# Attention scores over 32 rows per pair of heads, two pairs side by side, masks two units in a row, eight score buffers

## The reference

```
x = x + Wproj . softmax(mask(q k / 4)) v + bproj      q from layernorm(x), k and v from ctx, 16 heads of 16
x = x + out_proj(ssm(silu(conv(in_proj(layernorm(x))))) * silu(z))     a selective scan, state 16, 512 channels
x = x + down(quant(silu(gate) * up))                   gate, up, down with ternary weights, inputs rounded to 127 steps
```

## Time and profile before

| | us |
|---|---|
| median of 3 runs (lowest, highest) | 548.01 (546.25, 551.74) |
| the profiled execution's own time | 548.35 |
| its span | 546.3 |
| PE busy, share | 454.2, 83% |
| DVE busy, share | 404.0, 74% |
| POOL busy, share | 301.4, 55% |
| ACT busy, share | 246.4, 45% |

### The profile page before, as it was taken

How to read it: one execution, slowest core, us unless ns; L and a number is a source line. 1 busy time by engine, 2 the same in 40 slices (tenths; PEclk the granted TensorE clock), 3 DMA queues, 4 the chain that set the end, 5 groups by cost and what they waited for, 6 DMA issues and landing times.

```text
span 546.3 us, 9183 instructions
## 1 busy us (share of the span) xinstructions
PE 454.2 (83%) x3133; PEld 322.9 (59%) x3138; DVE 404.0 (74%) x779; ACT 246.4 (45%) x539; POOL 301.4 (55%) x310
## 2 busy tenths in 40 slices
PE   4999999999999797656696879998699989575563
PEld 1677777877767563345463647666578766453332
DVE  1376666767669898236979887798887799958994
ACT  1256546465764434582332446738243451223331
POOL 0564866747565625209763557799776689401100
PEclk9999999999999798977788899999799999998877
DMA  8910101101000000082000000173000000000000
GB/s 298 397 41 2 40 1 41 38 2 40 2 1 0 2 1 2 14 246 71 0 1 0 1 0 24 38 175 99 0 2 1 1 0 1 2 1 19 20 20 19
DMA packets 22769, 22.72 MB, mean 42 GB/s; under 512 B 1058, under 2 KB 20258, under 8 KB 22212
## 3 DMA queue, kind: packets, MB, share of 16 engines
q1 hardware_dynamic: 22164, 21.65, 12.5%
q10 hardware_dynamic: 560, 0.50, 0.3%
HBM read 21.03 MB, written 1.12 MB: 41 GB/s over the span
## 4 chain that ended last, share of the span: by engine, by line
PE 36%; POOL 19%; DVE 19%; issue 17%; ACT 3%; DMA 2%; DVEq 0%; POOLq 0%; SPq 0%; ACTq 0%
POOL both L1556 14%; PE ps L474 8%; DVE both L1281 5%; PE ps L483 4%; PE ps L538 3%; PE ps L511 3%; PE ps L714 3%; PE ps L704 3%; PE ps L499 3%; POOL both L1544 2%; PE ps L732 2%; DVE f_s L1381 2%; PE ps L378 1%; PE ps L570 1%; DVE both L1115 1%
## 5 line engine op out<-in xcount | busy, mean ns | idle before, releaser
L1556 POOL TENSOR_TENSOR both<-both 128x1024 f32<-128x1024 f32 x64 | 152.0, 2390 | 69.6 <-DVE both L1281 69.5
L1281 DVE TENSOR_TENSOR_SCAN both<-both,ps 128x1024 f32<-128x1024 f32 x64 | 145.1, 2280 | 33.0 <-PE ps L714 25.1
L945 ACT ACTIVATE both<-delta,a_neg 128x504 f32<-128x504 f32 x128 | 79.4, 706 | 52.1 <-DVE both L1281 52.0
L704 PE MATMUL ps<-both 64*128 64x256 f32 x512 | 77.6, 425 | 29.9 <-DVE both L1281 17.2
L844 ACT ACTIVATE both<-both,negmax 128x256 f32<-128x256 f32 x128 | 63.8, 502 | 65.3 <-DVE negmax L1115 65.2
L1505 POOL TENSOR_SCALAR both<-both,rden 128x256 f32<-128x256 f32 x128 | 63.7, 512 | 48.3 <-DVE rden L1122 48.0
L714 PE MATMUL ps<-con,both 128*128 128x128 f32 x512 | 74.2, 291 | 6.5 <-POOL both L1556 6.5
L704 PEld LDWEIGHTS ps<-both 64*128 64x128 f32 x512 | 47.5, 198 | 51.6 <-DVE both L1281 27.7
L714 PEld LDWEIGHTS ps<-con,both 128*128 128x128 f32 x512 | 58.3, 147 | 29.1 <-issue 15.8
L474 PE MATMUL ps<-both 128*128 128x256 f32 x256 | 70.4, 399 | 3.8 <-POOL both L1494 3.5
L1115 DVE CUSTOM_DVE_ANT_0 both<-ps,both 128x256 f32<-128x256 f32 x128 | 49.0, 420 | 16.7 <-PE ps L474 15.5
(11 more groups left out here) (130 smaller groups left out, 653.4 us busy)
## 6 DMA issues: line engine op xcount, KB each, us to landing
both<-bounce SPq DMA_DIRECT2D x16, 512.0 KB, 5.5
both<-in_ctx_t SPq DMA_DIRECT2D x8, 512.0 KB, 3.6
both<-in_wg SPq DMA_DIRECT2D x1, 1024.0 KB, 10.5
both<-in_wu SPq DMA_DIRECT2D x1, 1024.0 KB, 12.5
both<-in_wd SPq DMA_DIRECT2D x1, 1024.0 KB, 14.5
win_sb<-in_win SPq DMA_DIRECT2D x1, 1024.0 KB, 16.4
resid<-in_x SPq DMA_DIRECT2D x1, 896.0 KB, 8.9
both<-in_wkv SPq DMA_DIRECT2D x1, 512.0 KB, 4.0
```

What stands on the lines that cost most here:

```text
L704: mm = pe.matmul(out_v[:, :, s], ut[L * r:L * (r + 1), e.idx % 2, 2 * e.tt + s], bd[L * r:L * (r + 1), e.nh, e.tt, s * HN // 2 * L:(s + 1) ...
L945: act.activation(da[sl % 2].rearrange("p (a n s t) -> p a n s t", a=GT, n=HN, s=2)[:, :, n, :, 1:L], delta[:, idx % RING_X].rearrange("p ( ...
L1281: dve.tensor_tensor_scan(h_sb[:, hu % RING_H], da[e.slot % 2][:, e.tt * HU:(e.tt + 1) * HU], bank(2 * (hu % 2), 2), 0.0, ALU.mult, ALU.add ...
L1556: pool.tensor_tensor(h, h, cb[:, e.nh, e.tt], ALU.mult).then_inc(g_ready, 1)
```

## The change

`scores` no longer contracts over 128 rows with zeros. The queries of a pair of heads sit in 32 rows; each matmul contracts these 32 rows (`q2[rows, ...]`, `kt_sb[rows, ...]`). A unit is now a half `hf = u // 4` and one pair of heads, with the two sequences `bb` as its two blocks. Units u and u+1 are made together, at even u, their matmuls alternating between two groups of 32 rows and between banks 0 and 1; they wait for the masks of the pair before. `spread_queries` and `qbd` are gone; `copy_queries` writes the query twice, times 0/1 columns that leave one head of each pair (two instructions instead of one). VectorE masks units u and u+1 in a row at even u. Masked scores, maxima and sums have 8 buffers. `values` runs twice a tile with 16 matmuls each, at u = 6 and at u = 2 of the next tile, instead of four times with 8; `pt_sb` has two sets of four. `rstds(0)` on GpSimd moves from u = 2 to u = 1. In tile 6 the matmul of the weights' sums goes ahead of the scores. In the diff the first `body` is TensorE's, the second VectorE's, and `spread_queries` is GpSimd's.

```
-LAG_TURN, LAG_VALUES = 1, 2
+LAG_TURN, LAG_VALUES = 1, 3
-POOL_RSTD0, POOL_BIAS, POOL_RSTD1, POOL_RSTD2, POOL_SPREAD0 = 2, 3, 4, 6, 3
-POOL_SPREAD1 = 5
+POOL_RSTD0, POOL_BIAS, POOL_RSTD1, POOL_RSTD2 = 1, 3, 4, 6
...
             def scores(tile, u):
-                bb, hf, jj = u // 4, (u // 2) % 2, u % 2
+                hf = u // 4
                 if u == 0:
-                    pe.wait_ge(qbd_ready, count(tile.t * 2 + 2))
-                    pe.wait_ge(k_sb[0], count(tile.t + 1))
-                if u == 2:
-                    pe.wait_ge(k_sb[1], count(tile.t + 1))
-                pe.wait_ge(masked, count(tile.t * 16 + (2 * u - 2)))
-                for q in range(2):
-                    j = 2 * jj + q
-                    mm = pe.matmul(bank(u % 2)[:, q * LK:(q + 1) * LK], qbd[:, tile.par, bb, hf, j * P:(j + 1) * P],
-                                   kt_sb[:, tile.par, hf, bb * LK:(bb + 1) * LK], start=True, stop=True)
-                mm.then_inc(s_ready, 1)
+                    pe.wait_ge(q2_ready, count(tile.t * 2 + 2))
+                if u % 4 == 0:
+                    pe.wait_ge(k_sb[hf], count(tile.t + 1))
+                pe.wait_ge(masked, count(tile.t * 16 + 2 * u))
+                for bb in range(2):
+                    for v in (u, u + 1):
+                        rows = slice(32 * (v % 4), 32 * (v % 4) + 32)
+                        mm = pe.matmul(bank(v % 2)[:, bb * LK:(bb + 1) * LK],
+                                       q2[rows, tile.par, hf, bb].rearrange("p r q -> p (r q)"),
+                                       kt_sb[rows, tile.par, hf, bb * LK:(bb + 1) * LK], start=True, stop=True)
+                        if bb == 1:
+                            mm.then_inc(s_ready, 1)
...
             def values(tile, u):
-                pe.wait_ge(pt_in_sb[0], count(tile.t * 4 + (u // 2 + 1)))
-                pe.wait_ge(pt_in_sb[1], count(tile.t * 4 + (u // 2 + 1)))
-                for kt in range(2):
-                    for j in range(4):
+                pe.wait_ge(pt_in_sb[0], count(tile.t * 4 + 2 * hf + 2))
+                pe.wait_ge(pt_in_sb[1], count(tile.t * 4 + 2 * hf + 2))
+                for bb in range(2):
+                    for kt in range(2):
+                        for j in range(4):
...
             def body(tile, first, last, weights):
-                    if u < UNITS - 2:
-                        scores(tile, u + 2)
-                    elif not last:
-                        scores(nxt, u + 2 - UNITS)
...
+                    if u % 2 == 0 and u < UNITS - 2:
+                        scores(tile, u + 2)
+                    elif u % 2 == 0 and not last:
+                        scores(nxt, 0)
...
             def copy_queries(tile):
-                dve.tensor_scalar(qt[:].rearrange("p k t -> p (k t)"), bank(6)[:, 0:D], -QSCALE, None, ALU.mult
-                                  ).then_inc(q_sb, 1)
+                dve.wait_ge(s_ready, count(tile.t * 8 - 8))
+                for r in range(2):
+                    dve.tensor_scalar(q2[:, tile.par, :, :, r], bank(6)[:, 0:D].rearrange("p (k b q) -> p k b q", k=KD, b=2),
+                                      con[:, CON_PAR + r:CON_PAR + r + 1], -QSCALE, ALU.mult, ALU.mult
+                                      ).then_inc(q2_ready, 1)
...
             def exps(tile, u):
-                act.wait_ge(rden_ready, count(tile.t * 8 + (u - 3)))
+                act.wait_ge(rden_ready, count(tile.t * 8 + (u - 7)))
...
             def body(tile, first, last, weights):
-                    mask_scores(tile, u)
+                    if u % 2 == 0:
+                        mask_scores(tile, u)
+                        mask_scores(tile, u + 1)
...
-            def spread_queries(tile, halves):
-                pool.wait_ge(q_sb, count(tile.t + 1))
-                pool.wait_ge(s_ready, count(tile.t * 8 - 8))
-                for hf in halves:
-                    pool.tensor_tensor(
-                        qbd[:, tile.par, :, hf].rearrange("p b (h q) -> p b h q", h=8),
-                        qt[:, hf].rearrange("p (b q) -> p b q", b=2).unsqueeze(2).broadcast_to([P, 2, 8, L]),
-                        con[:, CON_HEAD:CON_HEAD + 8].unsqueeze(1).unsqueeze(3).broadcast_to([P, 2, 8, L]),
-                        ALU.mult).then_inc(qbd_ready, 1)
```

More of the change, by code:

```diff
@@ L163, in build @@
-        ctx_sb = first_use(10240, 2048).rearrange("p (a k n) -> p a k n", a=2, k=KD)
-        maskf = first_use(12288, 1024).rearrange("p (a n) -> p a n", a=2)
-        pt_sb = first_use(13312, 2048).rearrange("p (u a q) -> p u a q", u=4, a=4)
-        wraw = [first_use(15360 + 2048 * n, 2048) for n in range(3)]
-        wkv_sb = first_use(21504, 1024).rearrange("p (k n) -> p k n", k=KD)
-        wq_sb = first_use(22528, 512).rearrange("p (k n) -> p k n", k=KD)
-        mask_sb = first_use(23040, 1024).bitcast(U8)
@@ new lines, in build @@
+        v_sb = first_use(9216, 2048).rearrange("p (a b k d) -> p a b k d", a=2, b=2, k=2)
+        ctx_sb = first_use(11264, 2048).rearrange("p (a k n) -> p a k n", a=2, k=KD)
+        maskf = first_use(13312, 1024).rearrange("p (a n) -> p a n", a=2)
+        pt_sb = [first_use(*x).rearrange("p (u a q) -> p u a q", u=4, a=4) for x in ((1024, 2048), (14336, 2048))]
+        wraw = [first_use(16384 + 2048 * n, 2048) for n in range(3)]
+        wkv_sb = first_use(22528, 1024).rearrange("p (k n) -> p k n", k=KD)
@@ L293, in lagged @@
                 return
-            if only is None or v % 2 == only:
+            if only is None or v % UNITS in only:
                 fn(tile if v >= 0 else tile.step(-1), v % UNITS)
@@ L534, in vals @@
                 else:
-                    pe.wait_ge(q_sb, count(tile.t + 1))
+                    pe.wait_ge(q2_ready, count(tile.t * 2 + 2))
                 for kt in range(2):
@@ L614, in body @@
                     lagged(tile, u, LAG_TURN, first, turn_probs)
-                    lagged(tile, u, LAG_VALUES, first, values, 1)
+                    lagged(tile, u, LAG_VALUES, first, values, (3, 7))
                     if last:
@@ L629, in _ @@
             scores(t0, 0)
-            scores(t0, 1)
             pe.wait_ge(loaded, N_LOADED)
@@ L638, in _ @@
             for u in range(UNITS, UNITS + LAG_VALUES):
-                lagged(t7, u, LAG_VALUES, False, values, 1)
+                lagged(t7, u, LAG_VALUES, False, values, (3, 7))
             def x_proj(g, c, k, free):
@@ L829, in copy_vals @@
                 act.wait_ge(v_ready[0], count(tile.t + 1))
-                act.wait_ge(pv_done, count(tile.t * 4 - 4))
+                act.wait_ge(pv_done, count(tile.t * 2 - 2))
                 act.activation(v_sb[:, tile.par, 0].rearrange("p k d -> p (k d)"), bank(5), ACT.Copy
@@ L863, in body @@
                     exps(tile, u)
-                    lagged(tile, u, LAG_COPY_EVEN, first, copy_pt, 0)
+                    lagged(tile, u, LAG_COPY_EVEN, first, copy_pt, (0, 2, 4, 6))
                     if not last:
@@ L973, in _ @@
             for u in range(UNITS, UNITS + LAG_COPY_EVEN):
-                lagged(Tile(0, NT - 1), u, LAG_COPY_EVEN, False, copy_pt, 0)
+                lagged(Tile(0, NT - 1), u, LAG_COPY_EVEN, False, copy_pt, (0, 2, 4, 6))
             copy_gates(0, 2, 5)
@@ L1158, in body @@
                 for u in range(UNITS):
-                    mask_scores(tile, u)
+                    if u % 2 == 0:
+                        mask_scores(tile, u)
+                        mask_scores(tile, u + 1)
                     lagged(tile, u, LAG_INVERT, first, invert_sums)
-                    lagged(tile, u, LAG_COPY_ODD, first, copy_pt, 1)
+                    lagged(tile, u, LAG_COPY_ODD, first, copy_pt, (1, 3, 5, 7))
                     if not last:
@@ L1519, in body @@
                     normalise(tile, u)
-                    if u == POOL_SPREAD0 and not last:
-                        spread_queries(nxt, [0])
-                    if u == POOL_SPREAD1 and not last:
-                        spread_queries(nxt, [1])
             def pool_resid(tile):
@@ L1532, in _ @@
             rstds(0, t0)
-            spread_queries(t0, range(KD))
             pool.wait_ge(loaded, N_LOADED)
@@ L1616 @@
         np.eye(P),
-        head[:, None] // HD == np.arange(8)[None],
         head[:, None] // HD % 2 == np.arange(2)[None],
```

91 lines of the change are left out of this document (43 added, 48 removed).

## The result

The changed kernel takes 531.7 us (median of 4, 531.2 to 533.1) where the kernel before takes 548.4 (546.25 to 551.74): a ratio of 0.969, 95% interval 0.964 to 0.975. The medians differ by 16.7 us and the profiled executions (548.35 and 533.1) by 15.3, where 19.8 were forecast. A repeat gave 530.4, ratio 0.967 (0.962 to 0.971). The span of the profiled execution is 531.3. Medians are over all executions of a kernel, while ratios and their intervals leave out those more than 1.5% above its fastest.

The account below looks back on a forecast made before the run. TensorE was taken to bound regular tiles, VectorE tile 6. From 548.35 us, 3.6 (start and tile 0), 9.2 (tiles 1 to 4), 1.7, 4.5 and 0.8 (tiles 5, 6, 7), together 19.8, gave 528.5; range 519 to 540.

Parts of the forecast that it names:

- changing over, around a visit: TensorE's transposes ahead of the scores: 0.14 us more per visit, taken from the transposes ahead of L704.
- the price of a visit: TensorE's scores of two units: 1.06 + 0.14 = 1.20 us, priced from L704; 2.56 less a tile.
- the new waits in a regular tile: TensorE waits 0.3 us at `project` for `pick_heads` and 0.2 at `scan_in` for `norm_z`.
- PE idle ... none before L474: Expected sign on TensorE: idle of 0.2 to 0.5 us before L548 and L555, none before the scores.
- The least cover between two visits: TensorE's other work between two visits: at least 2.5 us, against 1.6 for a pair's masks.
- Tile 6: VectorE sets the time: 26.75 us of work taken for the tile's 31.25, so 4.5 less; bounds 2 and 6.5.
- +0.6: Tile 7's end: sixteen more records of `values` behind the last copy add 0.6 us, leaving the tile 0.8 less.
- Behind attention: What follows tile 7: 323.18 us, same lines and operands, so no change.
- what the buffers and GpSimd's work are worth: Regular tile: eight buffers instead of four and removing GpSimd's spreading were each worth zero, as neither ended a wait.
- the one without overlap: Scores: 32-row pairs do not overlap, a visit costs 2.07 us, a tile 24.0, the kernel 548.9; chance 6 in 100.
- The slower one, VectorE's queue as the bound: At `mask_scores`: VectorE's waits for scores grow, a tile takes 25.9 us, the kernel 558; chance 5 in 100.
- The rival in which the clock falls in regular tiles: Granted clock 0.89 in regular tiles: 23.1 us each, tiles 1 to 5 give nothing, kernel 539.2; chance 5 in 100.

Follow-up runs that it names:

- one row group: Changed kernel with every score matmul on rows 0 to 31, or on rows 0 to 63 (other scores than asked for): 557.5 and 549.6 us.
- the product: Changed kernel with GpSimd's old instruction put back as dead work, two products of 128 x 1024 a tile at u = 3 and 5: 548.9 us, ratio 0.998.
- the masks apart: Changed kernel with VectorE masking one unit per iteration again, TensorE still making scores two units at a time: 561.3 us, ratio 1.022.

## Why the prediction was right, and where it was short

By its steps, the profiled execution of before against that of after:

| step | forecast | measured |
|---|---|---|
| a visit of scores, to the next start | 1.06 | 1.06 |
| changing over, around a visit | 0.14 | 0.09 ahead, 0.11 behind |
| values, 32 records | 1.00 | 1.01 |
| regular tile | 20.6 | 20.71 |
| start and tile 0 (first keys of tile 1: 43.36 to 41.18) | 3.6 less | 2.2 less |
| tiles 1 to 4 | 9.2 less | 8.7 less |
| tile 5 | 1.7 less | 2.2 less |
| tile 6 | 4.5 less | 4.4 less |
| tile 7 | 0.8 less | 0.8 more |
| behind attention | 0 | 1.6 more |

**Right: the price of a visit.** L704 gave it to the hundredth, rows 64 or 32, and the experiments show why this was the right row: what it shares with the scores is that two row groups work at once. Inside a visit the trace agrees with the Trainium skill's rule (TensorE: Matmul & The Clock Gate, "Measured speedup vs the span model"), by which two such matmuls cost as one: the second record of a pair starts 6 to 7 ns behind the first, in L471 and in L704 alike, and a pair takes the 0.216 of a single record. The prediction set L704's 1.20 against that rule; what it had there was the price of going in and out of a visit, 0.19 inside it and 0.20 around it, and so its price stands. A whole visit is cheaper by 1.8 (1.06 against 1.92 in one row group, with the same 0.2 around both).

**Right: the new waits in a regular tile.** 0.3 at `project` and 0.2 at `scan_in` were forecast, 0.2 and 0.40 came.

**Short: "PE idle ... none before L474", at the start.** The least cover between two visits was worked out for a regular tile. In tile 0 nothing stands in TensorE's queue between the first two visits, so all of the masks' time shows: 1.79, and half clock behind it costs 0.5 in the scores and 1.1 in the keys, 3.4 together. Only 1.4 is missing there, so 2.0 came from what the forecast had not counted, and that is luck. Some 0.5 of it is that one step of `values` falls in tile 0 in place of three of four; 0.65 is two waits of the kernel before that are gone (0.24 ahead of its second scores, 0.41 ahead of `queries`); 0.8 is not accounted for. That the cover is missing was to be read in the program; that the clock can fall on it, from the earlier trace rows, where 2.50 of waiting did the same.

**Tile 6, right by other terms.** The 4.4 was to come from VectorE's 26.75 of work with no idle time. It was busy 25.07 and idle 1.8, half of the difference in work being that fewer of its mask instructions fall between the cuts (16 where there were 18, 0.85 less). And TensorE has a wait that the prediction did not list, 3.46 ahead of `scan_in`, with half clock behind it.

**Short: tile 7, "+0.6".** Up to the sixth `in_proj` the forecast held: it comes 21.54 after the cut (172.22 to 193.76) where it came 22.66 after it (189.68 to 212.34), 1.1 less for 1.4. From there to L643 it is 1.9 more, not 0.6. Of these, 0.9 is `values`: 32 more of its records stand there now, where the prediction counted 16. The rest, some 1.0, is half clock that lasts longer: through L569, `scan_in` and a turn, where before it ended with L570. That the single wait of 4.51, in place of 1.30 and 1.83, would take the clock with it for so long was not seen. Moving the turn and the values into the wait brought 1.6 back, so what it holds up is shown; that less work for TensorE made the wait longer is read from the trace alone.

**Behind attention** nothing is different between the kernels, and yet the profile has 324.82 against 323.18. The repeat of the changed kernel, windows view:

```profile
208.15:525.80 317.65, 245.89 (x1770) 171.91 (x1766) 249.89 (x267) 133.63 (x195) 177.62 (x101) 0.93 0.13 32
```

317.65, at a granted clock of 0.93 instead of 0.91. So the same instructions differ by 7 us between two executions; over all kernels here, none of which touches them, they took 316 to 326. The 1.6 belongs to that, not to the change. The difference in the total must be read with this in mind. That in attention, 16.64 (223.12 to 206.48), is the firmer number, though it too is 15.0 with the repeat (208.15). Against the first profile the miss is 19.8 less 16.64, 3.2: 1.4 at the start, 1.6 in tile 7, 0.5 in tiles 1 to 4 and 0.1 in tile 6, less 0.5 that tile 5 gave over its forecast.

**Right in the sum, wrong in a step: what the buffers and GpSimd's work are worth.** The prediction gave both zero in a regular tile, measured against the kernel before, where neither ended a wait. In the new order they do: four buffers cost 2.06 a tile, the product 1.03 and the clock. The chain through `norm_z` had been counted with GpSimd free, so the sum came out, but "zero" was the wrong price for leaving the part out. **Of the rivals**, the one without overlap gave 548.9 with a tile of 24.0; made real it took 549.6 on 64 rows and 557.5 on 32, both with a tile of 23.67. The slower one, VectorE's queue as the bound, is nearest to the kernel with the masks apart, where TensorE waits for the second mask. That 561.3 is close to its 558 is chance: its tile was to be 25.9 and is 23.23, and the rest is the clock and tiles 6 and 7. The rival in which the clock falls in regular tiles did not come in the changed kernel (1.00), but did with GpSimd's product back (0.93); its sum comes to 539.4 (548.35 less 3.6, 4.5 and 0.8), not 539.2.

## What to carry to other kernels

Price a packed matmul from a row in which two row groups work at once, count what each visit pays for going in and out (0.4 here, beside 0.87 of work), and look at the work between two such visits in the first and the last round, not only in a middle one. Parts of a change that remove no wait now may be what keeps the new order from making one: ask of each what would end last without it. A wait on TensorE can cost twice, once itself and once in the half clock behind it (after one of 1.8 in six of seven executions, after two of 0.6 in two of three), so when its queue is shortened, the waits that grow are to be listed too.

## What the runs showed of the hardware

- Two fp32 matmuls on two row groups cost as one while they run: their records start in pairs, 6 to 14 ns apart, and a pair takes 0.216, as a single record does. Each run of such pairs costs 0.19 more inside it and 0.20 around it.
- Overlap of row groups does not need the program to alternate between them: four records on one group and then four on the other took 1.07, as when alternated (1.06), and one group alone 1.92. The Trainium skill (TensorE: Matmul & The Clock Gate, "The mechanism") says that matmuls start and end strictly in program order. By it the second unit could not begin until the first one's fourth record had, so the visit would take the 0.87 of one unit and 0.65 (3 x 0.217) more, 1.52. The trace does not agree: the fourth record of the program starts 14 ns from the eighth.
- Contracting over 32 or 64 rows instead of 128 makes a single fp32 matmul no shorter: its records start 0.216 apart in all three.
- Half clock behind a short wait is not certain: the same instructions behind the same wait ran at full clock in one execution and at half in another. A wait of 1.42 in each tile left the granted clock at 1.00 in one tile and at 0.93 in the next. The total of that one kernel varied over 541.7 to 552.2, at mean granted clocks of 0.932 and 0.912.
